# Rotary step of an attention and FFN kernel: the sine product taken out of PSUM by VectorE, across the halves

## The reference

```python
def _rope(t, pos):
    d = t.shape[-1]
    half = d // 2
    inv_freq = ROPE_THETA ** (-jnp.arange(half, dtype=jnp.float32) / half)
    ang = pos[:, None].astype(jnp.float32) * inv_freq[None, :]
    cos = jnp.cos(ang)[None, :, None, :]
    sin = jnp.sin(ang)[None, :, None, :]
    t1, t2 = (t[..., :half], t[..., half:])
    return jnp.concatenate([t1 * cos - t2 * sin, t1 * sin + t2 * cos], axis=-1)
...
xn = _layernorm(x, axis=-1)
s = _L0_attn_ref(xn, L0_attn_wq, L0_attn_wk, L0_attn_wv, L0_attn_wo)
g = _silu(_L0_ffn_ref(xn, ...))
x = x + s * g
```

## Time and profile before

| | before |
|---|---|
| median of three runs | 989.2 us (986.09 to 992.18) |
| span of the profiled execution | 989.3 us; a time of it apart from the span is not listed |
| granted TensorE clock, mean | 0.976 |
| TensorE busy | 928.8 us (94%) |
| VectorE busy | 603.0 us (61%) |
| GpSimd busy | 517.3 us (52%) |
| ScalarE busy | 483.6 us (49%) |

### The profile page before, as it was taken

The page is one execution under the profiler, slowest core; times in us unless marked ns, Lnnn a source line. Parts: engine busy times, 40 slices in busy tenths (PEclk is TensorE's granted clock), DMA queues, the critical chain, the costliest instruction groups (busy, mean ns, idle before and its releaser), DMA issues. The chain is left out here.

```text
span 989.3 us, 15379 instructions
## 1 busy us (share of the span) xinstructions
PE 928.8 (94%) x4576; PEld 774.1 (78%) x4576; DVE 603.0 (61%) x1492; ACT 483.6 (49%) x1097; POOL 517.3 (52%) x397
## 2 busy tenths in 40 slices
PE   4799999999999999999999999999989798898896
PEld 3588888888888888888888888887867686686675
DVE  7757666656656566665666656566744544645646
ACT  5556556656565666566566566555331221221213
POOL 4557646556664765665576565652242432523525
PEclk9989999999999999999999999999999899899988
DMA  7002001110100111011020001013252624515432
GB/s 231 19 25 65 22 22 36 40 33 12 52 21 21 42 32 32 21 42 32 11 64 21 22 21 32 0 34 83 78 148 76 192 66 125 172 45 165 127 117 85
DMA packets 84300, 61.37 MB, mean 62 GB/s; under 512 B 3632, under 2 KB 71472, under 8 KB 84272
## 3 DMA queue, kind: packets, MB, share of 16 engines
q1 hardware_dynamic: 83552, 59.91, 20.7%
q10 hardware_dynamic: 720, 1.11, 0.3%
HBM read 58.92 MB, written 2.10 MB: 62 GB/s over the span
## 5 line engine op out<-in xcount | busy, mean ns | idle before, releaser
L51 PE MATMUL ps<-xt_hi,w_lo 128*128 128x512 f32 x608 | 238.4, 392 | 3.2 <-ACT sil L270 1.8
L52 PE MATMUL ps<-xt_lo,w_hi 128*128 128x512 f32 x608 | 237.8, 391 | 0.0
L53 PE MATMUL ps<-xt_hi,w_hi 128*128 128x512 f32 x608 | 237.6, 391 | 0.0
L678 ACT ACTIVATE probs<-probs,neg_max 128x256 f32<-128x256 f32 (+1 forms) x256 | 120.3, 471 | 86.1 <-DVE neg_max L909 86.1
L786 POOL TENSOR_TENSOR work<-work,sin 128x512 f32<-128x512 f32 x80 | 104.4, 1305 | 99.9 <-ACT work L660 99.8
L51 PEld LDWEIGHTS ps<-xt_hi,w_lo 128*128 128x128 f32 x608 | 114.8, 189 | 26.8 <-issue 2.2
L53 PEld LDWEIGHTS ps<-xt_hi,w_hi 128*128 128x128 f32 x608 | 114.4, 188 | 24.5
L52 PEld LDWEIGHTS ps<-xt_lo,w_hi 128*128 128x128 f32 x608 | 114.7, 189 | 22.5
L924 DVE TENSOR_TENSOR pt_lo<-ps,pt_hi 128x512 fp32r<-128x512 f32 (+1 forms) x64 | 69.7, 1089 | 75.7 <-ACT pt_hi L684 75.7
L918 DVE TENSOR_SCALAR probs<-probs,inv 128x256 f32<-128x256 f32 (+1 forms) x256 | 114.2, 509 | 2.3
L794 POOL TENSOR_TENSOR work<-work 128x512 f32<-128x512 f32 x75 | 97.0, 1293 | 25.4 <-DVE work L898 17.6
(11 more groups left out here) (82 smaller groups left out, 1782.9 us busy)
## 6 DMA issues: line engine op xcount, KB each, us to landing
work<-L_attn_wq SPq DMA_DIRECT2D x32, 256.0 KB, 2.8
work<-L_attn_wo SPq DMA_DIRECT2D x32, 256.0 KB, 2.6
work<-L_ffn_gate_w SPq DMA_DIRECT2D x14, 256.0 KB, 3.6
work<-L_ffn_gate_z SPq DMA_DIRECT2D x14, 256.0 KB, 4.5
work<-L_ffn_gate_s SPq DMA_DIRECT2D x14, 256.0 KB, 5.5
work<-L_ffn_up_w SPq DMA_DIRECT2D x14, 256.0 KB, 3.3
work<-L_ffn_up_z SPq DMA_DIRECT2D x14, 256.0 KB, 4.1
work<-L_ffn_up_s SPq DMA_DIRECT2D x14, 256.0 KB, 5.1
```

What stands on the lines that cost most here:

```text
L51: pe.matmul(out, stat[1], mov[0], start=first, stop=False)
L52: pe.matmul(out, stat[0], mov[1], start=False, stop=False)
L53: return pe.matmul(out, stat[0], mov[0], start=False, stop=last)
L678: act.activation(probs[:, h, cols], probs[:, h, cols], ACT.Exp, scale=-1.0, bias=neg_max[:, h:h + 1], accum_out=total[:, h:h + 1]).then_in ...
```

## The change

VectorE takes over the crosswise move and the sine product. For each tile it multiplies the upper 64 partitions of the PSUM bank by the sine table into the lower 64 partitions of `roped`, then the lower 64 into the upper 64, then takes the cosine product of all 128 as before. ScalarE's two copies and GpSimd's product go, and with them the buffer `swap` and its semaphore. The sine table is stored with the sign at the half it is read from. VectorE now waits for the projection itself, and for the split two tiles back (`rope_split`), since it writes `roped`. TensorE's and SyncE's instructions are the same.

```diff
-            def swap_halves(unit, b, i):
-
-                par = (5 * b + i) % 2
-                act.wait_ge(proj_ready, unit * PROJ + (i + 1))
-                wait(act, rope_sum, unit * 5 + (i - 1))
-                src = bank(b, i)
-                act.activation(swap[0:P // 2, par, :], src[P // 2:P, :], ACT.Copy)
-                act.activation(swap[P // 2:P, par, :], src[0:P // 2, :], ACT.Copy).then_inc(swapped, 1)
...
-            def times_sin(unit, b, i):
+            def rotate(unit, b, i):
 
                 par = (5 * b + i) % 2
-                pool.wait_ge(swapped, unit * 5 + (i + 1))
-                wait(pool, rope_split, unit * 5 + (i - 1))
-                pool.tensor_tensor(roped[:, par, :], swap[:, par, :], sin[:, :], ALU.mult).then_inc(sin_part, 1)
-
-            def rotate(unit, b, i):
-
-                par = (5 * b + i) % 2
-                times_sin(unit, b, i)
                 pool.wait_ge(sin_part, unit * 5 + (i + 1))
                 pool.wait_ge(proj_drained, unit * PROJ + (i + 1))
                 pool.tensor_tensor(roped[:, par, :], roped[:, par, :], direct[:, par, :], ALU.add).then_inc(rope_sum, 1)
...
-            pool.wait_ge(table_in, 48)
             for p in range(2, 6):
                 weight_lo(pool, 0, p)
             for i in range(5):
-                times_sin(0, 0, i)
-                if i > 0:
-                    lo_of_roped(0, 0, i - 1)
-            lo_of_roped(0, 0, 4)
+                lo_of_roped(0, 0, i)
...
             def cos_part(unit, b, i):
-                dve.wait_ge(swapped, unit * 5 + (i + 1))
-                wait(dve, rope_sum, unit * 5 + (i - 1))
-                dve.tensor_tensor(direct[:, (5 * b + i) % 2, :], bank(b, i), cos[:, :],
-                                  ALU.mult).then_inc(proj_drained, 1)
+                par, half = (5 * b + i) % 2, P // 2
+                dve.wait_ge(proj_ready, unit * PROJ + (i + 1))
+                wait(dve, rope_split, unit * 5 + (i - 1))
+                dve.tensor_tensor(roped[0:half, par, :], bank(b, i)[half:P, :], sin[half:P, :], ALU.mult)
+                dve.tensor_tensor(roped[half:P, par, :], bank(b, i)[0:half, :], sin[0:half, :],
+                                  ALU.mult).then_inc(sin_part, 1)
+                dve.tensor_tensor(direct[:, par, :], bank(b, i), cos[:, :], ALU.mult).then_inc(proj_drained, 1)
...
-        "rope_sin": np.concatenate([-sin, sin]),
+        "rope_sin": np.concatenate([sin, -sin]),
```

More of the change, by code:

```diff
@@ L367, in attention_block @@
     raw = [sh.work[:, s, :] for s in range(RING)]
-    swap, direct, roped = (sh.work[:, Shared.ROPE_AT + 2 * i:Shared.ROPE_AT + 2 * i + 2, :] for i in range(3))
+    direct, roped = (sh.work[:, Shared.ROPE_AT + 2 * i:Shared.ROPE_AT + 2 * i + 2, :] for i in range(1, 3))
     xin = y
@@ L426, in attention_block @@
         v_hi_done = sem("v_hi_done")
-        swapped = sem("swapped")
         sin_part = sem("sin_part")
@@ L710, in _ @@
                 weight_hi(act, 0, p)
-            swap_halves(0, 0, 0)
             root_of_var(1)
@@ L715, in _ @@
             act.activation(preload[:, 0:1], root[:, 0:1], ACT.Exp)
-            swap_halves(0, 0, 1)
             hi_of_roped(0, 0, 0)
-            swap_halves(0, 0, 2)
             hi_of_roped(0, 0, 1)
@@ L721, in _ @@
             hi_of_roped(0, 0, 2)
-            swap_halves(0, 0, 3)
             hi_of_roped(0, 0, 3)
-            swap_halves(0, 0, 4)
             for p in range(6, 8):
@@ L738, in body @@
                         n = g * 8 + (4 * b + j)
-                        if ahead and j == 0:
-                            swap_halves(un, bn, 0)
                         hi_of_probs(n, j)
@@ L751, in body @@
                             hi_of_roped(un, bn, 0)
[L752 to L756, removed]
                         if not ahead:
@@ L763, in body @@
                             hi_of_roped(un, bn, (1, 2, 4)[j])
-                        if ahead and j == 1:
-                            swap_halves(un, bn, 3)
                         if not last:
```

## The result

| | before | after |
|---|---|---|
| median of 13 runs each, same chip, by turns | 989.3 us (986.09 to 992.18) | 993.47 us (990.14 to 996.51) |
| ratio after / before | | 1.0037, 95% interval 1.0024 to 1.0051 |
| profiled execution: its own time, span | span 989.3 us | 993.2 us, 991.3 us |
| granted TensorE clock, mean | 0.976 | 0.978 |

The account below looks back on a forecast made before the run. The prediction took TensorE, busy 94% of the span and 99.65% in the loop, as the bound. It summed 989.3 + 0 (loop) - 1.1 (ahead of the loop) + 0 (FFN) = 988.2, said 988 us, range 983 to 997.

Parts of the forecast that it names:

- Costs of a tile: VectorE, each rotary tile: three products of 0.70 us, 2.10 instead of 0.60 us, +120 us over 80 tiles.
- the gain of the normalising: VectorE normalising heads in stage 2: about 0.9 us saved as one collision with GpSimd's sine product goes.
- VectorE fits in stage 2: End of stage 2 in the loop: VectorE needs 4.90 us of 5.02 us, so it fits by 0.1 us.
- The slow rival: Stage 2: VectorE late, output projection 0.8 us later in 15 units, +12 us, 1000 us (to 1010); chance 0.13.
- The loop at 0: Loop over the units: no change in time, VectorE's added work hidden behind TensorE, 99.65% full.
- Ahead of the loop: Part before the loop: terms -1.0, +1.2, -0.3 and -1.0 us, sum -1.1 us, bounds -4 to +1.5.
- The transposes: Ahead of the loop: TensorE's transposes of the second token half begin about 1 us earlier.
- the value's projection: Ahead of the loop: starts 1.2 us later, since VectorE releases its bank later.
- the value's turn: Ahead of the loop: no longer waits for ScalarE's queue, together with the last tile returning some 0.3 us.
- The normalising beside the weight splits: Ahead of the loop, at 47.06 us: two of four GpSimd splits over before it, -1 us from 3.46.
- the slow clock between 27 and 31.5 us: Ahead of the loop, TensorE's clock of 0.62 after idleness: a shorter slow stretch only in the -4 us bound.
- "+ 0 (FFN)": FFN behind the loop: no change in time, as it has no rotary step.

Follow-up runs that it names:

- k1: Changed kernel with tiny one-column instructions on ScalarE where its removed copies stood; 1.0014 times the kernel before.
- k2: Changed kernel repeated without further edits, a third time, on the same chip as k1; 1.0021 times the kernel before.
- g1: Changed kernel with the dropped semaphore allocated again and 33 one-column memsets on GpSimd ahead of the loop; 1.0003 times the kernel before.
- g2: Changed kernel with an unused 1 MiB array declared ahead of all others; 1.0002 times the kernel before.
- h4: Changed kernel with its inputs declared in reverse order; 1.0005 times the kernel before.

## Why the prediction was wrong

- **Costs of a tile: right.** 0.70 us for each product, taken between 0.60 and 0.79; measured 0.69 to 0.72. VectorE's busy time rose by 82 us, where +120 less the gain of the normalising was named: 160 new products of 0.69 us are 110 us of it, and the normalising gave 22 back (114.2 to 92.1).
- **The rule that the prediction cites**: the Trainium skill, page "VectorE: DVE Perf Modes", section "Two Vector instructions with no wait between them", has an instruction that starts in another group of 32 partitions than the one before it held until the earlier ones are finished. The trace agrees: the three products start 0.70 and 0.72 us apart, about their duration of 0.69, where reads of the same partitions (335.19 to 335.79) follow after 0.60.
- **VectorE fits in stage 2: right.** The heads took 1.45 us (1.6 said), the value's drain ended at 335.87 (335.8 said), and the output projection started with the 0.15 us of idleness of before. The slow rival, with 0.13, did not occur.
- **The loop at 0: right**, 558.00 for 558.04 us.
- **Ahead of the loop: the sum right, its terms off, so in part by luck.** The transposes came 1.4 us earlier (1.0 said); the value's projection started 1.5 us later (1.2 said). TensorE's wait of 1.52 us for the value's turn (at 41.09 before) is gone (0.3 said). The normalising beside the weight splits should have won 1 us and did not: the four heads take 3.38 us (3.46 before), since two of the four splits, at 47.27 now, still run beside them. Instead the slow clock between 27 and 31.5 us was gone, which I had left to the bound. In sum -1.0 us in the profile and -1.4 us in the runs without the FFN, for -1.1.
- **The step that failed: "+ 0 (FFN)"**, for which the text gives only that it has no rotary step. In the profile it took 3.0 us more, 2.9 of them in its five pairs (197.4 to 200.3); the repeated profiles of both kernels have 197.8 against 199.7 and 200.2. With the attention part at -1.4 us, the runs' 989.3 x 0.0037 = +3.7 us would put 5 us on the FFN, and the later sessions' +2.0 and +2.1 some 3.5. The prediction read what its engines do, and in the aligned pair that was indeed unchanged to the hundredth of a microsecond in the first 14 us; it never asked whether what follows would keep its times, the transfers and the instructions that run beside each other. The profile of before showed that this stage is not full: TensorE stands idle there for 22.4 us, waiting for VectorE's accumulation, at a mean clock of 0.93.
- That later landings come with ScalarE's shorter program is shown (k1 against k2, g1 against both). That they make the FFN slower is not: g1, g2 and h4 land late and are not slower, and in the aligned pair (24.66 against 25.25 us at the accumulation) most of the difference lies in L161 beside a product of GpSimd. The cause of the slower FFN stays open.
- Still open: what in ScalarE's program matters. Its length may move other things in the chip's memory; no run looked at that. A load by instructions being fetched in the loop of the FFN is unlikely: over the five pairs the traces hold two transfers of instructions in k1 and three in k2. A text of 289 instructions was enough and one of 279 was not; I did not try numbers between, nor a program filled up after the attention part. Open as well is why an edit elsewhere (33 `memset`s on GpSimd with a semaphore in g1, an array declared first in g2, the order of the arrays in h4) takes the slower FFN away.
- The chances: the range of 983 to 997 holds 993.47, and within 1% was the likeliest case. The direction was wrong, because I gave the gain of 1 us a sign and the untouched stage none. The prediction also took 9.9 us as about what a measurement can tell here; 13 runs of each kernel told +3.7 us from nothing, with 2.4 us as the lower end.

## What to carry to other kernels

A stage that a change does not touch can still change: here, where TensorE waits behind other engines and its granted clock is not full, the same FFN took 262.6 to 269.2 us under edits elsewhere, so such a stage gets bounds of its own in the sum (here some -1 to +5 us), and not a zero. Where a forecast gain is smaller than that, say no change and leave the sign open. To separate such an effect from the edit itself, run the changed kernel with tiny instructions where the removed ones stood, and time the stage itself in the profile, since the totals of a few runs cannot tell 2 us. A sign that goes with the edit, as the landing did, still has to be held against the time of the stage in every run before it is called the cause.

## What the runs showed of the hardware

- Products on VectorE that read the other 64 partitions of a PSUM bank take as long as straight ones (693, 684 and 692 ns for L863, L864 and L866, 80 each). Start to start they cost 0.70 us, not 0.60.
- VectorE's small instruction beside GpSimd's product fell from 1.19 to 0.17 us once that product was gone, and four heads from 2.53 to 1.45 us; but its products from PSUM stayed at 0.69 us throughout. In the FFN, VectorE's product of two operands in SBUF (L161) lasted 0.69 us in one pair and 1.63 beside a product of GpSimd in another.
- The same transfers of the FFN landed 0.7 us later in the mean with a ScalarE program of 279 instead of 289 to 339 instructions (16.5 against 15.85 us; 4.0 to 4.4 against 3.6 to 3.7 us for `gate_w`). With the order of the inputs reversed the one profile has 16.78. The later landing alone did not make the FFN slower.
- Of the FFN's 90 pairs in eighteen profiles, those with a mean granted clock of 0.95 or 0.96 took 37.7 to 39.2 us, those with 0.91 or 0.92 took 39.4 to 41.0. TensorE's wait for the accumulation was 4.2 to 5.0 us a pair in the mean of each profile, and 5.4 at most.
